# Indirect gathers and accumulating stores of a graph network, issued with and without an index limit

## The reference

```python
edge_index = stack([src, dst])
h = maximum(layernorm(x), 0)
x = x + L0(h)      # msg = W[type] @ h[src], segment_sum over dst, 6250 nodes of 8 rows
h = maximum(layernorm(x), 0)
x = x + L1(h)      # two rounds over all edges:
#   w   = relu(edge_attr @ w1 + b1) @ w2 + b2         per edge, 48 -> 320
#   msg = products of w with h[dst] and the edge's direction
#   out = segment_mean(msg, src), then batch norm; round two uses round one's rows
```

## Time and profile before

| | |
|---|---|
| median of three runs | 27402.51 us |
| the profiled execution, span from first to last instruction | 27406.8 us |
| POOL busy | 21912.9 us, 80% |
| TensorE busy | 15506.7 us, 57% |
| DVE busy | 14306.2 us, 52% |
| ACT busy | 8810.7 us, 32% |
| accumulating stores of rounds A and B | 13312 |
| accumulating stores of layer 0 | 104 |
| gathers of layer 0 | 832 |

### The profile page before, as it was taken

The page is one execution under the profiler, slowest core; times in us unless marked ns, Lnnn a source line. Parts: engine busy times, 40 slices in busy tenths (PEclk is TensorE's granted clock), DMA queues, the critical chain, the costliest instruction groups (busy, mean ns, idle before and its releaser), DMA issues.

```text
span 27406.8 us, 424599 instructions
## 1 busy us (share of the span) xinstructions
PE 15506.7 (57%) x111937; PEld 9860.4 (36%) x111937; DVE 14306.2 (52%) x29064; ACT 8810.7 (32%) x24449; POOL 21912.9 (80%) x14335
## 2 busy tenths in 40 slices
PE   4225666555556655655662555555555555555554
PEld 2223333333333333333331333333333333333332
DVE  5135555555555555555555555555555555555555
ACT  1003333333333333333331333333333333333332
POOL 2758888888888888888884888888888888888886
PEclk9557777777777777777776777777777777777776
DMA  6224444444444444444443333333333333333333
GB/s 197 48 74 59 59 59 58 59 59 59 59 59 59 58 59 59 59 58 59 59 58 88 55 55 55 54 55 55 55 55 55 55 55 55 55 55 55 55 55 59
DMA packets 3212288, 1687.49 MB, mean 62 GB/s; under 512 B 2559186, under 2 KB 2581330, under 8 KB 3208788
## 3 DMA queue, kind: packets, MB, share of 16 engines
q0 software_dynamic: 1970048, 277.58, 22.2%
q1 hardware_dynamic: 1235140, 1393.37, 17.5%
q10 hardware_dynamic: 7056, 16.06, 0.2%
HBM read 1394.67 MB, written 290.75 MB: 61 GB/s over the span
## 4 chain that ended last, share of the span: by engine, by line
POOL 47%; issue 29%; DMA 20%; DVE 2%; POOLq 1%; PE 1%; SPq 0%; ACT 0%; ACTq 0%; DVEq 0%
POOL accB L470 22%; POOL accA L470 21%; DMA accA<-arena 10%; DMA accB<-arena 8%; POOL arena L465 3%; DMA z_tab<-arena 1%; PE bank L634 0%; POOLq L173 0%; PE bank L636 0%; DMA arena<-accA 0%; DVE arena L1237 0%; DVE stat L1259 0%; POOLq L590 0%; POOL acc L470 0%; POOLq L504 0%
## 5 line engine op out<-in xcount | busy, mean ns | idle before, releaser
L709 PE MATMUL wide<-w,arena 128*128 128x320 f32 x26624 | 11743.2, 588 | 10004.1 <-DVE arena L1147 10002.4
L470 POOL DMA_INDIRECT accB<-arena x6656 | 10411.5, 1564 | 2359.9 <-issue 1939.6
L470 POOL DMA_INDIRECT accA<-arena x6656 | 10436.9, 1568 | 2203.2 <-issue 1922.0
L709 PEld LDWEIGHTS wide<-w,arena 128*128 128x128 f32 x26624 | 6172.6, 252 | 13435.8 <-DVE arena L1147 11312.4
L1147 DVE TENSOR_TENSOR arena<-wide,arena 128x640 f32<-128x640 f32 x6656 | 5474.4, 823 | 6564.0 <-POOLq L587 4178.9
L850 ACT CAST arena<-arena 128x272 bf16<-128x272 f32 (+3 forms) x3328 | 1187.4, 357 | 14825.3 <-DVE arena L1161 9365.1
L1154 DVE TENSOR_REDUCE arena<-arena 128x40 f32<-128x640 f32 (+1 forms) x6656 | 5244.9, 809 | 0.0
L857 ACT ACTIVATE arena<-arena 128x128 f32<-128x128 uint16 x13312 | 4229.0, 392 | 0.0
L1130 DVE TENSOR_TENSOR arena<-arena 128x96 f32<-128x96 f32 x832 | 216.1, 260 | 3878.8 <-POOLq L587 3878.8
L866 ACT ACTIVATE arena<-arena,ones 128x1024 bf16<-128x1024 f32 x1664 | 1915.2, 1151 | 0.5
L699 PEld LDWEIGHTS bank<-arena 128*128 128x128 bf16 x39936 | 1472.1, 108 | 1193.4 <-issue 1185.2
(11 more groups left out here) (127 smaller groups left out, 5353.8 us busy)
## 6 DMA issues: line engine op xcount, KB each, us to landing
arena<-src SPq DMA_DIRECT2D x1664, 256.0 KB
arena<-rel SPq DMA_DIRECT2D x1664, 256.0 KB
arena<-in_attr SPq DMA_DIRECT2D x3328, 96.0 KB
accA<-arena POOLq DMA_INDIRECT x6656, 3.2
accB<-arena POOLq DMA_INDIRECT x6656, 3.1
arena<-side SPq DMA_DIRECT2D x1664, 16.0 KB
arena<-accA SPq DMA_DIRECT2D x16, 1568.0 KB, 11.5
accA<-zero POOLq DMA_DIRECT2D x36, 640.0 KB, 54.4
```

The source lines that it names most:

```text
L470: pool.indirect_dma_start(out=tab, out_offset=bass.IndirectOffsetOnAxis(ap=idx, axis=0), in_=src_, in_offset=None, bounds_check=last_row[t ...
L709: last = pe.matmul(wide[k % 2][:, j, 0:WN], hT[:, s % 2, k * P:(k + 1) * P], w2_sb[r][:, j * WN:(j + 1) * WN], start=True, stop=True)
```

## The change

Both helpers issue their indirect transfers without the register of the limit and without the error flag. The four registers and the table of them go. Every indirect transfer of the program passes through one of the two helpers. In the built programs, apart from the four register loads at the start, POOL has the same number of instructions in the same order (each transfer with the companion instruction that belongs to an indirect one, before and after); what differs in a transfer is the field that names the limit register and the flags of the limit.

```diff
         @block.gpsimd
         def _(pool):
 
-            last_row = {rows: pool.to_reg(rows - 1) for rows in sorted({NP0 * NT, NP, NP0 + P, NP + P})}
-
             def gather(dst_, tab, idx, signal):
                 pool.indirect_dma_start(out=dst_, out_offset=None, in_=tab,
-                                        in_offset=bass.IndirectOffsetOnAxis(ap=idx, axis=0),
-                                        bounds_check=last_row[tab.shape[0]], oob_is_err=True).then_inc(signal, 16)
+                                        in_offset=bass.IndirectOffsetOnAxis(ap=idx, axis=0)).then_inc(signal, 16)
 
             def add_rows(tab, src_, idx, signal):
                 pool.indirect_dma_start(out=tab, out_offset=bass.IndirectOffsetOnAxis(ap=idx, axis=0),
-                                        in_=src_, in_offset=None, bounds_check=last_row[tab.shape[0]],
-                                        oob_is_err=True, compute_op=ALU.add).then_inc(signal, 16)
+                                        in_=src_, in_offset=None, compute_op=ALU.add).then_inc(signal, 16)
```

## The result

The changed kernel takes 27340.88 us (median of 12 runs, 27334.39 to 27344.36) against 27401.15 us (27390.24 to 27410.69, 12 runs): a ratio of 0.9978, with a 95% interval of 0.9971 to 0.9986. It is faster by 60 us, 0.22%. I had forecast 26833 us, a gain of 570. The stated range, 25900 to 27700, held the measured time, but it is wide enough to hold "no gain" too, so that says little for the working.

A forecast was written before the change was run, and what follows sets the result against it. POOL, issuing 14248 indirect transfers one after the other, was taken as the bound. 14248 x 0.040 = 570 us off 27407 gave 26837, and 26833 as the span stands 4 us above the median; range 25900 to 27700.

The forecast's parts named there:

- POOL is the bound, and a nanosecond in a transfer comes through in full: 14248 transfers run one after the other on POOL; a nanosecond in each is 14.25 us of the span, 0.05%.
- The cover, 9.2 us a group: In the rounds, other engines need 9.2 us a group against POOL's 14.9; POOL could lose 5.7 before they set the pace.
- The register loads cost nothing: At the start, the four register loads take 0.07 us in all, hidden under DVE's preparation.
- 40 ns, for stores and gathers alike: Each of 14248 indirect transfers gains 40 ns, the root of 17 x 96: 570 us in all.
- The size in a gather: Each of the 832 gathers gains 40 ns, its median falling from 1013 to some 970 ns.
- The division of 481 ns into five steps of a row: A gather's 481 ns of work above a plain transfer, taken as five row-by-row steps, the limit being one: 96 ns.
- The upper end of 96 ns: Largest gain used for each of the 14248 transfers: 1368 us, 5.0%.
- The rival "no change", second form: Stores' limit may not be on the slower side; at most 832 gathers gain, 33 us; "no change" in all 30%.
- The rival "no change", first form: Transfers compare the limit in any case, or in free slots of the row loop: no gain; "no change" in all 30%.
- The rival "slower": Without the flag each of 14248 transfers takes a general way, 17 to 96 ns longer: 27645 to 28770 us; 20%.
- The likeliest case's own range: Span of times for the faster case, 50%, around 26833 us: 26000 to 27340.

The follow-up runs named there:

- the rounds without addition: Kernel before and changed kernel, each with stores of rounds A and B replacing rows instead of adding: 19911.33 us with the limit, 19582.78 without.
- half of the stores: Kernel before, with POOL issuing only the stores of tiles 0 to 3 of each group in rounds A and B: 16716.67 us.
- the kernel that kept the loads: Kernel before with only the 832 gathers of layer 0 losing the limit, stores keeping it: 27341.66 us against 27400.14, ratio 0.9978.

## Why the prediction was wrong, step by step

- **POOL is the bound, and a nanosecond in a transfer comes through in full.** Right. The gathers gave 62.4 us of busy time, and round A began 62.8 us earlier. Where stores do pay for the limit it held nearly: in the rounds without addition its removal cut POOL's busy time by 295.9 us and the rounds by 267.5. One sentence of the working doesn't fit its own rows: a landing does not end "about when POOL would have been ready anyway", but 3.1 us after an issue that lies 7.45 us back, and the idle time before rows that name it is the usual 0.30. The conclusion, no separate limit, stands.
- **The cover, 9.2 us a group.** Right in what it was used for; too cautious by 0.7 us, as half of the stores showed, as its pairs held waits for TensorE, whose granted clock was 0.74 there.
- **The register loads cost nothing.** Right: the first gather starts at 534.8 us, before at 534.7, and the kernel that kept the loads had the whole gain.
- **"40 ns, for stores and gathers alike".** This is the step that failed, and by far the largest part of the error. 13416 of the 14248 transfers are accumulating stores, and for them the term is 0: 13416 x 40 ns = 537 us of the forecast 570 did not exist. I had priced the store from the gather, though the rows showed that the two differ by 549 ns, and though I had written under the rivals that the limit may not show there.
- **The size in a gather.** Forecast 40 ns, measured 66 to 75 (33 us forecast, 62 measured). The division of 481 ns into five steps of a row was mistaken in kind: the gather of 16 rows already takes 892 of the 1010 ns, so only 118 ns of the transfer depend on the rows. Of the 476 ns by which a gather of 128 rows exceeds a plain load (1010 to 534; the 481 of the prediction was a fair reading) at least 358 are then there at 16 rows, if a plain load of 16 rows takes no longer than one of 128; none was run. The upper end of 96 ns held all the same.
- **The rival "no change", second form**, had the outcome: the stores gain nothing and at most the gathers do. With the measured 75 ns instead of 40 it gives 832 x 0.075 = 62 us, which is the result; its own time, 27370 to 27403, lies above the measured one. Its reason was not the right one: it took the 549 ns between stores and gathers as a sign that the side with the index differs. An indexed store without addition takes 982 ns against a gather's 1010 and does pay, so the difference between stores and gathers comes with the addition, and it is the addition that decides. By the Trainium skill, "Perfetto Trace Analysis", section on the GPSIMD's DMA instruction, the recorded end of such a transfer is that of the last of two descriptor writers. What was measured fits this: with the addition an otherwise visible price goes to 0 or 8 ns. Whether one of the two writers has the side with the index, no run here shows.
- **The rival "no change", first form**, read from the earlier trace rows that no table size moves a store. The rows can't show that: `accA` and `accB` have the same number of rows and differ only in a row's length (32 and 16 floats).
- **The rival "slower"** fell: no kind of transfer was longer without the limit.
- **The range** ended at 27700 above and held the point where nothing is gained; but it stands on both signs. The likeliest case's own range, 26000 to 27340, just missed the measured 27340.88. Its upper end was to stand for 4 ns a transfer, which is 57 us and so 27346 us: worked out rightly, the case would just have held the result. That would have been luck, as 4 ns on every transfer is not what happened, but 75 on 832 of them and none on the rest.

What stays open: that the limit's time lies beside a slower side in an accumulating transfer is argued from the pattern, not seen, as the trace has one interval for both sides. Another reading, that additions go through other code that compares anyway or does so for nothing, fits zero at all row counts as well; the 8 ns of the accumulating gather are too small to decide. Nor is it settled why an indexed store pays 13 to 24 ns where a gather pays 52 to 66. A transfer with one side made slower by other means than an addition could tell the two apart; none was run.

## What to carry to other kernels

When an edit touches one helper that issues two kinds of operation, price the kinds apart, and give the kind that makes up 94% of the count a term of its own before giving it another's price; a difference of 549 ns between two kinds is a reason to ask what limits each. A price that is divided over rows must first be shown to depend on rows. And a gain of 7% in one operation is worth its count times its nanoseconds: here 832 gathers, 62 us of 27,400; for a kernel bound by gathers like these the same edit would, by my estimate, be worth 5% of each gather's period (66 of 1310 ns), where the indices are known to be valid.

## What the runs showed of the hardware that I had not expected

An indirect transfer of few rows costs POOL most of what one of many rows does: a gather without limit took 837 ns with 16 rows and 944 with 128, an accumulating store 1290 and 1552. In the stream 0.30 us of gap comes with each. The addition put 594 ns on an indexed store (958 to 1552) and 333 on a plain one (537 to 870). With half of the stores TensorE, which had waited for DVE and so for POOL, was granted 0.99 of its clock in round A instead of 0.74, without a change in its work.
